# Key parts stored once each, and the cyclic row of key parts made by five loads an operand instead of three loads from a doubled store

## The chip, the cores and the metric

The kernel runs on one core of a Trainium2 chip. The metric is the device time of one execution in microseconds, the median of several runs. A DMA is issued by an engine's queue (here nearly always SyncE's, "SPq" in the profile) and carried by the core's 16 DMA engines.

## The reference

One pre-norm decoder layer on x of [1, 1024, 128], with a context of [1, 6404, 128]:

```python
x = x + attn(layernorm(x))          # 16 heads of 8; k and v through a latent of 32; scores times
                                    # exp(-0.01*|t_q - t_k|), softmax, times v, times W_o
x = x + xattn(layernorm(x), ctx)    # q = x W^T + b; softmax(q ctx^T + (1 - mask) * -1e6) ctx
x = x + ffn(layernorm(x))           # fp4 block quantization of activations and weights, silu gate
```

The change lies in the first of the three. There q and k for all 16 heads are needed as operands of score matmuls with float32-like precision.

## The kernel before, in words

**Operands in three parts.** Queries and keys are scaled by a growing or a falling exponential of the position, so that the decay becomes a plain product on one side of the diagonal. This gives four operands: lower queries QL, lower keys KL, upper queries QU and upper keys KU. Each is split into three bf16 parts (high, middle, low), called parts 0, 1 and 2. One matmul over 112 partitions then multiplies a row of nine blocks of 8 partitions on either side: query parts 0,1,2 three times over against key parts in the cyclic order 0,1,2, 1,2,0, 2,0,1. The head dimension is 8, so a part of one head is 8 partitions, nine blocks are 72 partitions, and the rest hold constants and, later, three rows of softmax shifts.

**Through DRAM.** VectorE and ScalarE make the parts with (head, dimension) on 128 partitions, in the order KL, QL, QU, KU (lines 720, 733, 737, 537, 541). `store_parts` writes them to DRAM (`key_parts`, `query_parts`; lines 287 and 292). `load_operand(g, w)` (line 310) reads them back for a group g of four heads, now with 8 partitions a part and four heads times 1024 positions, 8 KB, along each partition. `load_first_queries` (line 321) does that for QL of group 0 in two halves of 512 positions. Two operand buffers alternate over the four groups. All of these are issued on SyncE's queue in the order in which the code is written; the waits there are on semaphores of the parts, of the stores' landing, and, for groups 2 and 3, on the scores of the group before last.

**Keys.** A load of 24 partitions takes three consecutive slots of `key_parts`. So that the cyclic order can be read this way, the DRAM tensor has five slots with parts 0,1,2,0,1: parts 0 and 1 are written twice. The three loads begin at slots 0, 1 and 2.

**What follows.** TensorE's first use of an operand is `max_unit(mu)`: for 16 units a half group (4 heads by 4 query tiles), in order of mu from 0 to 127, it computes 128x1024 scores (line 918), and VectorE multiplies them by the decay and takes the row maximum (line 744). The first 23 units run before any attention probability is made; with them TensorE also transposes the context (line 1051). From then on 32 "pairs" of score blocks, exponentials (ScalarE, line 609) and products with v (line 1027) run, each with four more units of maxima woven in. Units 0 to 31 are of group 0, 32 to 63 of group 1, and so on. The maxima of 16 units become shifts, stored by six small DMAs into the query operands (`load_shift`, line 335). Cross-attention and the feed-forward part come after all that.

TensorE waits for the first operands on one semaphore, `s_op0`: the three loads of KL and the three of QL's first half, 16 counts each.

Of the kernel before, what the change touches and what calls it, by code (L numbers as in the profile page):

```python
# [11 lines left out]
BF16 = mybir.dt.bfloat16  # L12
# [5 lines left out]
HEADS = 16  # L18
# [2 lines left out]
LN_EPS = 1e-5  # L21
BLOCK = 16
PARTS = 3
SLOTS = 2 * PARTS - 1
CLEAR_ROW = 64
ONES_PAIR = 1.0 + 127.0 * 2.0 ** -16
MATH_ROWS = 112
# [2 lines left out]
HG = 4  # L30
# [3 lines left out]
def decoder_layer(nc, x, ctx, mask, w_q, w_k, w_v, w_o, w_down_kv, w_up_k, w_up_v,  # L34
                  xw, xb, w_gate, w_up, w_down, out):
    S, D = x.shape[1], x.shape[2]
# [3 lines left out]
    HD = D // HEADS  # L40
    NT = S // P
    NG = HEADS // HG
    NH = S // BANK
# [31 lines left out]
    with ExitStack() as stack:  # L75
# [3 lines left out]
        def sem(name):  # L79
            return stack.enter_context(nc.semaphore(name))  # L80

        PS = stack.enter_context(nc.psum_tensor("banks", [P, 8, BANK], F32))

        k_scratch = nc.dram_tensor("key_parts", [2, SLOTS, HD, HEADS, S], BF16, kind="Internal").ap()
        q_scratch = nc.dram_tensor("query_parts", [2, NH, PARTS, HD, HEADS, BANK], BF16, kind="Internal").ap()

        ident = sb("ident", [P, P])
# [21 lines left out]
        with ExitStack() as first_stack:  # L109
            def sb0(name, shape, dt=F32):  # L110
                return first_stack.enter_context(nc.sbuf_tensor(name, shape, dt))
# [4 lines left out]
            parts_sb = sb0("operand_parts", [P, 4, PARTS, S], BF16)  # L116
# [8 lines left out]
        NB = 2  # L125
# [20 lines left out]
        def operand(buf, which):  # L146
            return ops[buf][:, which, :, :]
        QL, KL, QU, KU = range(4)
# [3 lines left out]
        def queries(buf, which, half):  # L152
            return ops[buf][:, which, :, :].rearrange("p h n -> p (h n)").rearrange(
                "p (a h n) -> p a h n", a=NH, h=HG)[:, half, :, :]
# [55 lines left out]
        s_op = [[sem(f"lower_operands_loaded_{b}") for b in range(NB)], [sem(f"upper_operands_loaded_{b}") for b in range(NB)]]  # L210
# [28 lines left out]
        def unit(b, i):  # L239
            half, pair, odd = b // NT, b % NT // 2, b % 2  # L240
            head = i // 2 + 2 * ((i + odd) % 2)
            on = i % 2 == 0
            return head, (half if on else 1 - half) * TPB + pair, half
# [3 lines left out]
        def max_slot(mu):  # L247
            return (mu + max(mu - 1, 0) // UNITS) % 2
# [10 lines left out]
        def chunk(c):  # L259
            return c * BANK, min(BANK, S2 - c * BANK)  # L260
# [15 lines left out]
        def _(sp):  # L276
# [5 lines left out]
            def store_parts(w):  # L282
                if w in (KL, KU):
                    for part, ready in ((0, s_hi), (1, s_mid), (2, s_lo)):
                        sp.wait_ge(ready, NH * (turn_of(w) + 1))
                        for slot in range(part, SLOTS, PARTS):
                            sp.dma_start(k_scratch[w // 2, slot].rearrange("d h n -> (d h) n"),
                                         parts_sb[:, w, part, :]).then_inc(s_scr[w], 16)
                    return
                for half in range(NH):  # L290
                    sp.wait_ge(s_lo, NH * turn_of(w) + half + 1)
                    sp.dma_start(q_scratch[w // 2, half].rearrange("a d h n -> (d h) a n"),
                                 parts_sb[:, w, :, half * BANK:(half + 1) * BANK]).then_inc(
                                     s_scr0 if w == QL and half == 0 else s_scr[w], 16)

            def load_operand(g, w):
                if g == 0:
                    sp.wait_ge(s_scr[w], 16 * (SLOTS if w in (KL, KU) else 1 if w == QL else NH))
                if g < NB:
                    sp.wait_ge(s_spare[g], 2 + 2 * g)  # L300
                if g == 0 and w in (QL, QU):
                    sp.wait_ge(s_qz, 2)
                for s in range(PARTS):
                    rows = operand(g % NB, w)[s * PARTS * HD:(s + 1) * PARTS * HD, :, :]
                    if w in (KL, KU):
                        src = k_scratch[w // 2, s:s + PARTS, :, g * HG:(g + 1) * HG].rearrange("a d h n -> (a d) h n")
                    else:
                        rows = rows.rearrange("p h n -> p (h n)").rearrange("p (a m) -> p a m", a=NH)
                        src = q_scratch[w // 2, :, :, :, g * HG:(g + 1) * HG].rearrange("f a d h n -> (a d) f (h n)")
                    sp.dma_start(rows, src).then_inc(s_op0 if g == 0 and w == KL else s_op[w // 2][g % NB], 16)  # L310

            def load_first_queries(half):
                sp.wait_ge(s_spare[0], 2)
# [44 lines left out]
            for hg in range(3, NG * NH):  # L358
                if hg % NH == 1 and hg // NH + 1 < NG:
                    g = hg // NH + 1  # L360
# [9 lines left out]
            for t in range(NT + 1):  # L370
                for m in range(NMP if t < NT else 0):
                    n = t * NMP + m
# [6 lines left out]
                    w = min(MP, S2 - m * MP)  # L379
# [127 lines left out]
        def _(act):  # L507
# [49 lines left out]
            def mem_high(c):  # L557
                k0, kw = chunk(c)
                act.wait_ge(s_mt, c + 1)
                if c == 0:  # L560
                    act.wait_ge(s_scr0, 16)
                    for w in range(4):
                        act.wait_ge(s_scr[w], 16 * (SLOTS if w in (KL, KU) else 1 if w == QL else NH))
                act.activation(memT_hi[:, k0:k0 + kw], PS[:, c % 4, 0:kw], ACT.Copy).then_inc(s_mhi, 1)

            def mem_low(c):
# [349 lines left out]
        def _(pe):  # L916
            def mm(o, a, b, start=True, stop=True, alone=False):
                return pe.matmul(o, a, b, start=start, stop=stop, skip_group_check=alone)  # L918
# [38 lines left out]
            def max_unit(mu):  # L957
                hg, h = mu // UNITS, mu % UNITS // TPB
                g, qt = hg // NH, hg % NH * TPB + mu % TPB
                if hg >= 1 and mu % UNITS == 1:  # L960
                    pe.wait_ge(s_mxd, mu)
                elif hg >= 1 and mu % UNITS == 2:
                    pe.wait_ge(s_sp, hg)
                elif mu >= 2:
                    pe.wait_ge(s_mxd, mu - 1)
                if mu % UNITS == 0 and hg % NH == 0:
                    if hg == 0:
                        pe.wait_ge(s_op0, 16 * 2 * PARTS)
                    else:
                        pe.wait_ge(s_op[0][g % NB], 16 * 2 * PARTS * (g // NB + 1) - (16 * PARTS if g % NB == 0 else 0))  # L970
                    pe.wait_ge(s_spare[g % NB], 2 + 2 * (g % NB))
                if mu == UNITS:
                    pe.wait_ge(s_op[0][0], 16 * PARTS)
                ql, kl = queries(g % NB, QL, hg % NH), operand(g % NB, KL)
                j = mu % TPB
                for i in range(NH):
                    last = mm(PS[:, 4 + 2 * max_slot(mu) + i, :], ql[0:MATH_ROWS, h, j * P:(j + 1) * P],
                              kl[0:MATH_ROWS, h, i * BANK:(i + 1) * BANK])
                last.then_inc(s_mx, 1)
# [5 lines left out]
            def scores(n, j):  # L985
                u = n * PU + j
                gb = 2 * n + j // HG % 2
                g, b = gb // BLKS, gb % BLKS
                if j == 0 and gb % NT == 0:
                    hg = gb // NT  # L990
                    if b == 0:
                        pe.wait_ge(s_op[1][g % NB], 16 * 6 * (g // NB + 1))
                    pe.wait_ge(s_sh[hg % 2], 16 * 2 * PARTS * (hg // 2 + 1))
                if u >= 3:
                    pe.wait_ge(s_p, u - 2)
                bank = PS[:, u % 3, :]
                half = b // NT
                def side(kq, h, kt, cols, **more):
                    qs, ks = (QL, KL) if kq == "lower" else (QU, KU)
                    return mm(bank[:, cols] if kq != "diag" else bank[:, h * P:(h + 1) * P],  # L1000
                              operand(g % NB, ks)[0:FULL_ROWS, h, kt * P:(kt + 1) * P],
                              queries(g % NB, qs, half)[0:FULL_ROWS, h, cols], **more)
                if j == 2 * HG:
                    kt = half * TPB + b % NT // 2
                    d0 = kt % TPB * P
                    for h in range(HG):
                        last = side("diag", h, kt, slice(d0, d0 + P), start=(h == 0), alone=True)
                elif j % 2 == 1:
                    h, kt, _ = unit(b, j % HG)
                    last = side("lower" if kt < half * TPB else "upper", h, kt, slice(0, BANK))  # L1010
                else:
                    h, kt, _ = unit(b, j % HG)
                    d0 = kt % TPB * P
                    last = side("lower", h, kt, slice(d0, BANK))
                    if d0 > 0:
                        last = side("upper", h, kt, slice(0, d0), start=False, alone=True)
                last.then_inc(s_st, 1)
# [218 lines left out]
            for t in range(NT):  # L1236
                for c in range(NC):
                    probs_T(t, c)
                    n = (t + 1) * NC + LEAD + c
# [36 lines left out]
```

## Time and profile before

| | us |
|---|---|
| median of 3 runs (564.05 to 565.44) | 564.52 |
| the profiled execution | 563.12 |
| its span, in which all times below stand | 561.0 |
| TensorE busy in the span | 494.5 (88%) |
| VectorE busy | 366.3 (65%) |
| ScalarE busy | 334.5 (60%) |

Times in the profile are counted from the span's start. "Idle before" an instruction is put down to what ended it. A DMA's time is that of its issue on the queue; its data moves later. "DMA share" is the mean busy share of the 16 DMA engines in a stretch, GB/s what they moved. KB of a DMA are 1024 bytes: a load of 24 partitions by 8 KB is listed as 192.0 KB.

### The profile page before, as it was taken

How to read it: one execution, taken by the hardware profiler on the slowest of the kernel's cores; microseconds unless marked ns; L12 is line 12 of the kernel's file. 1: busy time of each engine (PE TensorE's matmuls, PEld its weight loads, DVE VectorE, ACT ScalarE, POOL GpSimd, SP SyncE). 2: the span in 40 equal slices, each digit the busy share in tenths (PEclk: the TensorE clock that was granted, in tenths of full speed). 3: DMA queues.
4: the chain of work that ended last, by engine and by line, in shares of the span. 5: the costliest groups of instructions: out<-in, count | busy, mean ns of one | idle time of the engine just before them, and what ended most of it. 6: DMA issues, size and time to landing. Idle time of an engine off the chain costs nothing.

```text
span 561.0 us, 9555 instructions
## 1 busy us (share of the span) xinstructions
PE 494.5 (88%) x3394; PEld 319.8 (57%) x3394; DVE 366.3 (65%) x874; ACT 334.5 (60%) x659; POOL 169.9 (30%) x283
## 2 busy tenths in 40 slices
PE   6539899999999999999879979799897997989953
PEld 5305433333333333323659979799797997878841
DVE  7789988888778878701674366646566565653543
ACT  3545777787878777889155827446272653628410
POOL 7800033544444453233443221312222132110000
PEclk9857999999999999999989989989899999989985
DMA  8787300052007000063565323233332434300000
GB/s 239 236 265 150 84 4 2 4 114 58 1 3 160 13 2 2 1 176 100 188 215 156 109 75 115 90 112 91 112 115 61 124 99 122 90 1 6 1 5 5
DMA packets 21810, 49.19 MB, mean 88 GB/s; under 512 B 3948, under 2 KB 9268, under 8 KB 21188
## 3 DMA queue, kind: packets, MB, share of 16 engines
q1 hardware_dynamic: 21012, 47.87, 30.3%
q8 instruction: 27, 0.44, 0.3%
q0 software_dynamic: 224, 0.54, 0.3%
q10 hardware_dynamic: 528, 0.18, 0.2%
q14 instruction: 19, 0.16, 0.1%
HBM read 43.67 MB, written 4.72 MB: 86 GB/s over the span
## 4 chain that ended last, share of the span: by engine, by line
PE 68%; DVE 21%; DMA 3%; issue 3%; ACT 2%; POOL 1%; SPq 1%; DVEq 0%; ACTq 0%; POOLq 0%
PE banks L918 47%; PE banks L1027 11%; PE banks L1172 6%; DVE banks L744 6%; DVE logits L825 3%; PE banks L1038 2%; DMA mring<-in_mask_BxSxS_ik 1%; DVE fa L861 1%; ACT probs L609 1%; DMA operands<-query_parts 1%; DMA x_sb<-in_x 1%; DVE xn L709 1%; PE banks L1220 1%; DVE qc_lo L791 1%; DVE fa L860 1%
## 5 line engine op out<-in xcount | busy, mean ns | idle before, releaser
L609 ACT ACTIVATE probs<-banks 128x512 f32<-128x512 f32 x288 | 158.9, 600 | 40.6 <-PE banks L918 34.8
L744 DVE CUSTOM_DVE_ANT_0 banks<-banks,decay 128x1024 f32<-128x1024 f32 x128 | 155.0, 1245 | 30.4 <-PE banks L918 29.8
L918 PE MATMUL banks<-operands 112*128 112x512 bf16 (+4 forms) x736 | 147.4, 332 | 20.9 <-DMA operands<-query_parts 13.5
L918 PEld LDWEIGHTS banks<-operands 115*128 115x128 bf16 (+1 forms) x736 | 55.1, 98 | 126.8 <-ACT probs L609 57.5
L918 PEld LDWEIGHTS banks<-mem,pT 128*128 128x128 f32 (+1 forms) x816 | 109.3, 197 | 7.9
L918 PE MATMUL banks<-mem,pT 128*128 128x128 f32 (+1 forms) x816 | 112.9, 282 | 0.0
L825 DVE CUSTOM_DVE_ANT_0 logits<-banks,mring 128x512 f32<-128x512 f32 (+1 forms) x102 | 67.5, 668 | 49.3 <-PE banks L918 25.0
L630 ACT ACTIVATE pT<-banks 128x512 f32<-128x512 f32 (+1 forms) x104 | 60.4, 580 | 53.0 <-PE banks L1172 53.0
L484 POOL TENSOR_SCALAR mring<-mring 128x1024 f32<-128x1024 int32 (+1 forms) x55 | 52.8, 959 | 85.1 <-DMA mring<-in_mask_BxSxS_ik 82.7
L465 POOL TENSOR_SCALAR_AFFINE_SELECT probs<-probs 128x128 f32<-128x128 f32 x128 | 37.1, 293 | 113.4 <-ACT probs L609 111.8
L1027 PE MATMUL banks<-probs,v_ext 128*32 128x512 f32 x512 | 68.2, 604 | 0.7 <-ACT probs L609 0.5
L918 PE MATMUL banks<-memT_hi,qc_hi 128*128 128x512 f32 (+1 forms) x104 | 50.0, 481 | 19.1 <-DVE cmax L825 19.1
L1172 PE MATMUL banks<-ident,logits 128*128 128x128 f32 (+1 forms) x408 | 63.7, 279 | 0.0
L620 ACT ACTIVATE logits<-logits,neg_max 128x1024 f32<-128x1024 f32 (+1 forms) x56 | 58.8, 1050 | 6.7 <-DVE neg_max L832 6.7
L1172 PEld LDWEIGHTS banks<-ident,logits 128*128 128x128 f32 (+1 forms) x408 | 49.8, 144 | 4.0 <-issue 2.2
L457 POOL TENSOR_TENSOR rstd<-mv,half_neg 128x1 f32<-128x1 f32 x16 | 8.8, 550 | 127.1 <-DVE mv L867 85.2
L918 PE MATMUL banks<-memT_hi,qc_lo 128*128 128x512 f32 (+1 forms) x104 | 41.5, 399 | 0.0
L918 PE MATMUL banks<-memT_lo,qc_hi 128*128 128x512 f32 (+1 forms) x104 | 41.0, 394 | 0.0
L918 PEld LDWEIGHTS banks<-memT_hi,qc_hi 128*128 128x128 f32 x104 | 20.7, 199 | 22.3 <-DVE cmax L825 21.6
L469 POOL TENSOR_SCALAR_AFFINE_SELECT probs<-probs 128x512 f32<-128x512 f32 x32 | 20.3, 635 | 41.1 <-ACT probs L609 41.1
L650 ACT ACTIVATE xqT<-banks 128x128 f32<-128x128 f32 x8 | 2.2, 277 | 37.9 <-PE banks L1209 37.9
L918 PEld LDWEIGHTS banks<-memT_hi,qc_lo 128*128 128x128 f32 x104 | 20.2, 194 | 4.4
(168 smaller groups left out, 482.4 us busy)
## 6 DMA issues: line engine op xcount, KB each, us to landing
mring<-in_mask_BxSxS_ik SPq DMA_DIRECT2D x47, 512.0 KB, 3.5
operands<-key_parts SPq DMA_DIRECT2D x24, 192.0 KB
operands<-query_parts SPq DMA_DIRECT2D x21, 192.0 KB
key_parts<-operand_parts SPq DMA_DIRECT2D x10, 256.0 KB, 3.7
query_parts<-operand_parts SPq DMA_DIRECT2D x4, 384.0 KB, 4.5
mring<-in_mask_BxSxS_ik SPq DMA_DIRECT2D x8, 130.0 KB, 2.3
operands<-shift_parts SPq DMA_DIRECT2D x48, 4.0 KB, 1.8
operands<-query_parts SPq DMA_DIRECT2D x6, 96.0 KB
```

The lines of the kernel that those rows point to most:

```text
L465: pool.affine_select(out=diag, in_=diag, compare_op=ALU.is_ge, fill=0.0, base=0, pattern=[[1, P]], channel_multiplier=-1).then_inc(s_sel, 1)
L469: pool.affine_select(out=upper, in_=upper, compare_op=ALU.is_ge, fill=0.0, base=-1, pattern=[[0, HG], [-1, P]], channel_multiplier=1).then ...
L484: pool.tensor_scalar(src.bitcast(F32), src, -1.0, -NEG, ALU.add, ALU.mult).then_inc(s_ma, 1)
L609: act.activation(probs[:, to, :], PS[:, u % 3, :], ACT.Exp).then_inc(s_p, 1)
L620: act.activation(y, y, ACT.Exp, bias=neg_max[:, t:t + 1], accum_out=esum[:, t, e:e + 1]).then_inc(s_e, 1)
L630: last = act.activation(pT[:, n % 3, 0:o], PS[:, 2 + n % 2, 0:o], ACT.Copy)
L744: dve.tensor_tensor_reduce(out=rows, in0=rows, in1=decay[:, off:off + S], scale=1.0, scalar=-3.0e38, op0=ALU.mult, op1=ALU.max, accum_out= ...
L825: dve.tensor_tensor_reduce(out=logits_sb(t)[:, k0:k0 + kw], in0=PS[:, logits_bank(n), 0:kw], in1=mk, scale=1.0, scalar=-3.0e38, op0=ALU.ad ...
L918: return pe.matmul(o, a, b, start=start, stop=stop, skip_group_check=alone)
L1027: last = pe.matmul(PS[h * VW:(h + 1) * VW, 3, :], v_ext[:, kt, g * HG + h, :], probs[:, (gb % 2) * HG + i, :], start=(b % NT == 0), stop=( ...
L1038: last = pe.matmul(PS[h * VW:(h + 1) * VW, 3, d0:d0 + P], v_ext[:, kt, g * HG + h, :], probs[:, 2 * HG + n % 2, h * P:(h + 1) * P], start= ...
L1172: last = pe.transpose(PS[0:kw, 2 + n % 2, j * P:(j + 1) * P], logits_sb(t)[:, k * P:k * P + kw], ident[:, :])
```

## The change

`key_parts` has three slots, one a part, and each part is stored once: for KL and KU three stores of 256 KB each where there were five. In `load_operand` for keys, the row of nine blocks is made by five loads: (row 0, parts 0,1,2), (row 24, parts 1,2), (row 40, part 0), (row 48, part 2), (row 56, parts 0,1). They fill 24, 16, 8, 8 and 16 partitions. Loads of queries stay as they are. The counts waited for are changed to match (8 loads for a pair of operands instead of 6).

```diff
 PARTS = 3
-SLOTS = 2 * PARTS - 1
+K_RUNS = ((0, 0, 3), (24, 1, 2), (40, 0, 1), (48, 2, 1), (56, 0, 2))
+LOADS = len(K_RUNS) + PARTS
...
-        k_scratch = nc.dram_tensor("key_parts", [2, SLOTS, HD, HEADS, S], BF16, kind="Internal").ap()
+        k_scratch = nc.dram_tensor("key_parts", [2, PARTS, HD, HEADS, S], BF16, kind="Internal").ap()
...
                         sp.wait_ge(ready, NH * (turn_of(w) + 1))
-                        for slot in range(part, SLOTS, PARTS):
-                            sp.dma_start(k_scratch[w // 2, slot].rearrange("d h n -> (d h) n"),
-                                         parts_sb[:, w, part, :]).then_inc(s_scr[w], 16)
+                        sp.dma_start(k_scratch[w // 2, part].rearrange("d h n -> (d h) n"),
+                                     parts_sb[:, w, part, :]).then_inc(s_scr[w], 16)
...
+                heads = slice(g * HG, (g + 1) * HG)
+                if w in (KL, KU):
+                    for row, part, n in K_RUNS:
+                        sp.dma_start(operand(g % NB, w)[row:row + n * HD, :, :],
+                                     k_scratch[w // 2, part:part + n, :, heads].rearrange("a d h n -> (a d) h n")).then_inc(
+                                         s_op0 if g == 0 and w == KL else s_op[w // 2][g % NB], 16)
+                    return
                 for s in range(PARTS):
-                    rows = operand(g % NB, w)[s * PARTS * HD:(s + 1) * PARTS * HD, :, :]
-                    if w in (KL, KU):
-                        src = k_scratch[w // 2, s:s + PARTS, :, g * HG:(g + 1) * HG].rearrange("a d h n -> (a d) h n")
...
-                        pe.wait_ge(s_op0, 16 * 2 * PARTS)
+                        pe.wait_ge(s_op0, 16 * LOADS)
```

On SyncE's queue, at the stores of KL and the first loads, these rows stood before (a row is line, destination <- source, partitions x elements, and how many in a row):

```order
L287 DMA key_parts<-operand_parts 128x1024 x5
L292 DMA query_parts<-operand_parts 128x3x512 x2
L310 DMA operands_0<-key_parts 24x4096 x3
L321 DMA operands_0<-query_parts 24x2048 x6
L292 DMA query_parts<-operand_parts 128x3x512 x2
```

and these now:

```order
L287 DMA key_parts<-operand_parts 128x1024 x3
L292 DMA query_parts<-operand_parts 128x3x512 x2
L306 DMA operands_0<-key_parts 24x4096
L306 DMA operands_0<-key_parts 16x4096
L306 DMA operands_0<-key_parts 8x4096 x2
L306 DMA operands_0<-key_parts 16x4096
L325 DMA operands_0<-query_parts 24x2048 x6
L292 DMA query_parts<-operand_parts 128x3x512 x2
```

Two stores are gone, and two more DMAs stand between the stores and the query loads; the order of everything else is the same.

On the same queue, at the loads of group 2 between the shifts of two half groups, there stood before:

```order
L335 DMA operands_1<-shift_parts 1x16x128 x6
L310 DMA operands_0<-key_parts 24x4096 x3
L310 DMA operands_0<-query_parts 24x2x2048 x6
L310 DMA operands_0<-key_parts 24x4096 x3
L335 DMA operands_1<-shift_parts 1x16x128 x6
```

and now:

```order
L339 DMA operands_1<-shift_parts 1x16x128 x6
L306 DMA operands_0<-key_parts 24x4096
L306 DMA operands_0<-key_parts 16x4096
L306 DMA operands_0<-key_parts 8x4096 x2
L306 DMA operands_0<-key_parts 16x4096
L312 DMA operands_0<-query_parts 24x2x2048 x6
L306 DMA operands_0<-key_parts 24x4096
L306 DMA operands_0<-key_parts 16x4096
L306 DMA operands_0<-key_parts 8x4096 x2
L306 DMA operands_0<-key_parts 16x4096
L339 DMA operands_1<-shift_parts 1x16x128 x6
```

Twelve loads have become sixteen, with the same bytes to the same partitions; the next group's shifts stand behind them as before.

## Rows read from the trace of the kernel before

**Rows 1.** The page: span and busy time of each engine.

```profile
span 561.0 us, 9555 instructions
PE 494.5 (88%) x3394; PEld 319.8 (57%) x3394; DVE 366.3 (65%) x874; ACT 334.5 (60%) x659; POOL 169.9 (30%) x283
```

**Rows 2.** The chain that ended last, 24 to 37 us: start, duration, what.

```profile
24.58 1.30 DVE operand_parts L737 x2
...
25.90 0.36 SPq L292
...
26.37 0.55 SPq L310
...
26.96 0.98 SPq L310
...
27.99 0.37 SPq L310
...
29.22 6.00 DMA operands<-query_parts
35.23 0.24 issue
...
36.64 1.23 DVE banks L744
```

**Rows 3.** The chain, 60 to 68 us.

```profile
65.69 1.12 DVE banks L744
...
66.93 1.04 PE banks L918 x4
```

**Rows 4.** TensorE's waits, 20 to 70 us: total, times, longest.

```profile
PE banks L918 <- DMA operands<-query_parts: 13.5, 1, 13.5
```

**Rows 5.** Busy time in stretches: each engine's, then PEclk, DMA share, GB/s.

```profile
4.00:12.00 8.00, 6.48 (x38) 5.44 (x36) 6.21 (x22) 4.67 (x10) 6.17 (x4) 1.00 1.09 290
...
25.00:26.00 1.00, 0.00 (x0) 0.00 (x0) 1.00 (x3) 0.14 (x1) 1.00 (x1) 1.00 0.00 0
36.00:38.00 2.00, 1.35 (x5) 0.16 (x3) 1.53 (x4) 0.00 (x0) 0.00 (x0) 0.50 1.07 379
43.00:46.00 3.00, 2.65 (x6) 0.49 (x5) 3.00 (x5) 0.00 (x0) 0.00 (x0) 0.50 0.82 161
57.00:58.00 1.00, 0.77 (x5) 0.33 (x4) 0.97 (x4) 1.00 (x3) 0.00 (x0) 1.00 0.00 0
119.00:131.00 12.00, 12.00 (x92) 4.24 (x87) 9.76 (x16) 9.74 (x18) 5.07 (x11) 1.00 0.75 165
```

**Rows 6.** SyncE's queue in order of time: start, duration, issues.

```profile
19.81 2.77 SPq L287 DMA_DIRECT2D key_parts<-operand_parts  x5
25.29 0.97 SPq L292 DMA_DIRECT2D query_parts<-operand_parts  x2
26.37 1.99 SPq L310 DMA_DIRECT2D operands<-key_parts  x3
28.47 2.34 SPq L321 DMA_DIRECT2D operands<-query_parts  x6
31.61 0.99 SPq L292 DMA_DIRECT2D query_parts<-operand_parts  x2
...
42.16 2.34 SPq L310 DMA_DIRECT2D operands<-key_parts  x6
44.54 1.19 SPq L310 DMA_DIRECT2D operands<-query_parts  x3
58.60 3.79 SPq L335 DMA_DIRECT2D operands<-shift_parts  x6
```

**Rows 7.** SyncE's queue, 115 to 190 us.

```profile
116.12 1.11 SPq L310 DMA_DIRECT2D operands<-key_parts  x3
117.69 2.38 SPq L310 DMA_DIRECT2D operands<-query_parts  x6
...
168.63 1.11 SPq L310 DMA_DIRECT2D operands<-key_parts  x3
169.78 2.43 SPq L310 DMA_DIRECT2D operands<-query_parts  x6
```

**Rows 8.** Line 744 alone from 36 us on (two instructions a unit).

```profile
36.00:131.40 95.40, 78.67 (x128) 0.94 0.34 82
36.00:131.60 95.60, 78.79 (x129) 0.94 0.34 82
```

**Rows 9.** The same to 184 us.

```profile
36.00:183.90 147.90, 118.91 (x192) 0.96 0.29 70
36.00:184.10 148.10, 119.02 (x193) 0.96 0.29 69
```

**Rows 10.** All waits of TensorE, 110 to 190 us.

```profile
PE banks L918 <- DVE row_max L744: 2.0, 4, 0.5
```

More of the change, by code:

```diff
@@ L297, in load_operand @@
                 if g == 0:
-                    sp.wait_ge(s_scr[w], 16 * (SLOTS if w in (KL, KU) else 1 if w == QL else NH))
+                    sp.wait_ge(s_scr[w], 16 * (PARTS if w in (KL, KU) else 1 if w == QL else NH))
                 if g < NB:
@@ L302, in load_operand @@
                     sp.wait_ge(s_qz, 2)
-                for s in range(PARTS):
-                    rows = operand(g % NB, w)[s * PARTS * HD:(s + 1) * PARTS * HD, :, :]
-                    if w in (KL, KU):
-                        src = k_scratch[w // 2, s:s + PARTS, :, g * HG:(g + 1) * HG].rearrange("a d h n -> (a d) h n")
[L307 to L310, printed above, removed]
+                heads = slice(g * HG, (g + 1) * HG)
[5 more added lines that the diff above has]
+                    return
+                for s in range(PARTS):
+                    rows = operand(g % NB, w)[s * PARTS * HD:(s + 1) * PARTS * HD, :, :].rearrange("p h n -> p (h n)")
+                    sp.dma_start(rows.rearrange("p (a m) -> p a m", a=NH),
+                                 q_scratch[w // 2, :, :, :, heads].rearrange("f a d h n -> (a d) f (h n)")).then_inc(
+                                     s_op[w // 2][g % NB], 16)
             def load_first_queries(half):
@@ L562, in mem_high @@
                     for w in range(4):
-                        act.wait_ge(s_scr[w], 16 * (SLOTS if w in (KL, KU) else 1 if w == QL else NH))
+                        act.wait_ge(s_scr[w], 16 * (PARTS if w in (KL, KU) else 1 if w == QL else NH))
                 act.activation(memT_hi[:, k0:k0 + kw], PS[:, c % 4, 0:kw], ACT.Copy).then_inc(s_mhi, 1)
@@ L967, in max_unit @@
                     if hg == 0:
-                        pe.wait_ge(s_op0, 16 * 2 * PARTS)
+                        pe.wait_ge(s_op0, 16 * LOADS)
                     else:
-                        pe.wait_ge(s_op[0][g % NB], 16 * 2 * PARTS * (g // NB + 1) - (16 * PARTS if g % NB == 0 else 0))
+                        pe.wait_ge(s_op[0][g % NB], 16 * LOADS * (g // NB + 1) - (16 * len(K_RUNS) if g % NB == 0 else 0))
                     pe.wait_ge(s_spare[g % NB], 2 + 2 * (g % NB))
@@ L991, in scores @@
                     if b == 0:
-                        pe.wait_ge(s_op[1][g % NB], 16 * 6 * (g // NB + 1))
+                        pe.wait_ge(s_op[1][g % NB], 16 * LOADS * (g // NB + 1))
                     pe.wait_ge(s_sh[hg % 2], 16 * 2 * PARTS * (hg // 2 + 1))
```

## The prediction

> **What bounds the kernel now.** I read the page first: TensorE is busy for 494.5 of 561.0 us [rows 1], so over most of the span a DMA costs nothing. Then the chain of work that ended last, because the changed DMAs matter only where it passes through them. It does so once. From 24.58 us on it runs through the last splits of QL on VectorE, the issue of the query stores, the three KL loads and the first query loads on SyncE's queue, and then 6.00 us of DMA, up to 35.23 [rows 2]. The table of waits says the same from TensorE's side: 13.5 us idle before its first score matmul, ended by the query loads, its only wait for a DMA between 20 and 70 us [rows 4]. From 36.64 us to 66.8 the chain is VectorE's maxima of line 744, one unit after the other, and then it is TensorE's [rows 2, 3]. So whatever moves the landing at 35.23 moves the rest of the kernel by as much: the units behind it are bound by VectorE, TensorE's work by their order, and nothing is made in advance meanwhile.
>
> **The removed stores.** Two stores of KL are gone from the issue at 19.81 [rows 6]. What did they hold up? Between 25 and 26 us the DMA engines moved nothing, share 0.00 [rows 5]: all five stores had drained before the first query store (issued 25.29) reached them, and that one waits for VectorE's split, not for the queue. The first KL load follows the second query store (25.90 + 0.36) at 26.37 with no wait for the landing of the key stores in between [rows 2]. So the two stores are worth 0 here. Without that cover (stores still draining at 25.3) they would be worth up to 2 x 262 kB at 379 GB/s, the rate of the store stretch at 36 to 38 us [rows 5], 1.4 us. The two stores of KU do lie in busy DMA time, and their 1.4 us lets the KU loads start earlier, but no one waits for those.
>
> **The two more issues an operand.** An issue of such a load takes 2.34 / 6 = 0.39 us (six from 42.16) [rows 6], so the query loads are issued 0.8 us later, from 29.3 instead of 28.47. The data of KL takes 3.6 us (below) and starts after the query stores' data, hence the query loads are issued well before their turn. Worth 0, and 0.8 us if there were no queue of data. Behind them on SyncE stands the store of QU, issued at 31.61; the last query load would now end at 30.81 + 0.8 = 31.6, just in time.
>
> **The five loads themselves.** This is the term that decides. The rows to read are the stretches with their DMA share. In 119 to 131 us only loads of 24 partitions are in flight: share 0.75, so about 12 of 16 engines are busy, and 165 GB/s; at 43 to 46 us it is 161 GB/s [rows 5]. A busy engine thus moves 165 / 12 = 13.7 GB/s. It is not that an engine can't do more: stores from all 128 partitions ran at 379 GB/s, 23.7 an engine, loads to 128 partitions (x and the context, 4 to 12 us) at 290, 18.1 an engine. What differs is the number of partitions that are written, so I read the 165 GB/s as 24 partitions at 6.9 GB/s each. By that a load of 8 KB a partition takes 196.6 kB / 165 GB/s = 1.19 us whether it has 24, 16 or 8 partitions, as long as loads go one after the other: three loads take 3.6 us, five take 6.0. **+2.4 us** on KL, and the first queries land behind it.
>
> The Trainium skill (SBUF — State Buffer, Door 1: The DMA port swizzle) states what would make this so: four neighbouring partitions, and the four 32 further on, share one of 16 ports of about 27 GB/s. By it 24 partitions have six ports, 163 GB/s, and the traces agree with 165 and 161; 8 partitions have two ports, 54 GB/s, so 65.5 kB take 1.2 us, and the sum would again be +2.4.
>
> Both ends for this term. Low: loads overlap, because an engine that is through with its rows goes on to the next load, which writes other partitions. If overlap were perfect the bytes are the same and the term is 0 (it could be -0.5 if the four engines idle before now carry rows of the 16-partition loads; more is excluded, since the low rate is not the engines'). High: engines get out of step, and the query loads behind, 0.6 us each by their 98 kB, suffer as well; doubling three of them adds 1.8, together +4.2. I take 2.4, since the measured loads before show no overlap: sustained over 12 us they never exceed the rate of one [rows 5].
>
> **Later loads.** Groups 2 and 3 are loaded under TensorE's work, and TensorE waits for no DMA in 110 to 190 us [rows 10]. Group 2: issue from 116.12 [rows 7]; six loads of KL and QL at 1.19 are 7.1 us, with about 2 us ahead of and behind the data some 125.3. They are needed at unit 64, which VectorE starts at 131.5 [rows 8] and TensorE about 1 us before: 5 us of margin. With the change KL costs 2.4 more, or 4.8 if QU's loads, running past QL's on engines that are ahead, slow QL by as much again: 0.2 to 2.6 us of margin stay. Group 3 is the same: issue 168.63, unit 96 at 184.0 [rows 7, 9]. Worth 0; if the cover is gone, 0.5 to 1.5 us each. The shifts of the first half group are issued at 58.60, with the DMA engines idle from 57 on [rows 5, 6]; KU and KL of the next group push that data 4.8 us later, plus 2.4, less 1.4 for KU's stores, to about 62.5, while the shifts are issued 61.0 to 64.8. The last of the six still finds the engines free. Worth 0.
>
> **Sum.** 0 + 0 + 2.4 + 0. The profiled execution took 563.12 (span 561.0 and 2.1 around it): 565.5. It lies 1.4 below the median of the runs, so I forecast 564.5 + 2.4 = **566.9**. What a measurement of this kernel tells from no change is 0.3%, 1.7 us.
>
> **Rivals.**
> - *Rows an engine, not partitions, set the time* (not slower). If the 12 busy engines carry two rows of 8 KB each of a 24-partition load, a load of 16 or 8 partitions gives an engine one row. Then the most loaded engines have 2 + 1 + 1 + 1 + 1 = 6 rows, as before with three loads of 2, and the time of KL is 3.6 us in both kernels. For it: the share of exactly 0.75. Against it: the 23.7 and 18.1 GB/s of an engine in other stretches. It decides if a row keeps taking 1.19 / 2 = 0.6 us in an 8-partition load; the time is 564.5. The Trainium skill (DMA: Bandwidth & Descriptors, Why a DMA increments its semaphore by 16 and not by 1) has this split: the number of engines is the largest up to 16 that divides the slowest dimension, 12 for 24 partitions, 16 for 16, 8 for 8; the share of 0.75 agrees. Taken alone it gives 564.5. 24%.
> - *The crowding spreads* (slower still). The query loads run out of step, +4.2, and the loads of groups 2 and 3 come 0.5 late each: 564.5 + 5.2 = 569.7. For it: margins of 0.2 to 2.6 us. Against: 5 us of margin before. 16%.
> - *The idle engines help.* The 16-partition loads use all 16 engines and the term is -0.5, with KU's stores gone too: 564.0. Against it: the rate of 24 partitions did not come from the engines. 10%.
> - The forecast itself, +1.2 to +3.5: 50%.
>
> **Chances and range.** Slower by over 0.3% (over 566.2): nearly all of the forecast's half and of the second rival, 0.61. Within: the first rival, the low edge of the forecast, most of the third, 0.33. Faster: 0.06, from the third and scatter. The range reaches from just under the first and third rivals, 564.1, to just over the second, 570.0.
>
> **What the profile of the changed kernel would show.** TensorE's wait before the first score matmul grows from 13.5 to about 15.9 us, line 744 begins at about 39.0 instead of 36.64, and the chain's DMA piece there is longer by 2.4 us. In the stretch from 29 to 34 us, GB/s falls well below 165, and the DMA share with it or not: a share that stays up at falling GB/s says that engines stand in line for partitions. The DMA engines are still idle between 25 and 26 us. No wait of TensorE for a DMA in 110 to 190 us. I am wrong if KL's data takes 3.6 us again (first rival), or if the maxima show a stall at units 64 or 96 (second).

## The result and the profile after

| | before | with the change |
|---|---|---|
| median of 20 runs each, us | 564.05 | 566.64 |
| ratio, 95% interval | | 1.004 (1.0025 to 1.0054) |
| span of the profiled execution, us | 561.0 | 565.4 |

The change costs 0.4%, by the ratio 2.3 us (1.4 to 3.0 by the interval); the two medians are 2.6 us apart. The spans differ by more than that, 4.4 us, and single executions of one kernel scatter by as much: the 20 runs of before lie between 560.55 and 566.65.

The page's sections on DMA show what was moved: 46.83 MB on SyncE's queue where before had 47.87, two parts less for KL and for KU, in 16 loads of 128 KB, 8 of 192 KB and 16 of 64 KB for the keys.

```profile
span 565.4 us, 9567 instructions
...
q1 hardware_dynamic: 20628, 46.83, 32.5%
...
HBM read 43.67 MB, written 3.67 MB: 84 GB/s over the span
...
operands<-key_parts SPq DMA_DIRECT2D x16, 128.0 KB
key_parts<-operand_parts SPq DMA_DIRECT2D x6, 256.0 KB, 3.4
...
operands<-key_parts SPq DMA_DIRECT2D x8, 192.0 KB
...
operands<-key_parts SPq DMA_DIRECT2D x16, 64.0 KB
```

SyncE's queue in order of time answers to [rows 6] (start, duration, issues; the key loads are line 306 now):

```profile
20.12 2.43 SPq L287 DMA_DIRECT2D key_parts<-operand_parts  x3
25.61 0.97 SPq L292 DMA_DIRECT2D query_parts<-operand_parts  x2
26.68 2.64 SPq L306 DMA_DIRECT2D operands<-key_parts  x5
29.43 2.35 SPq L325 DMA_DIRECT2D operands<-query_parts  x6
```

The chain that ended last, in 24 to 41 us, answers to [rows 2], and TensorE's first wait, in the second fence, to [rows 4]. The last two have TensorE's first score matmul, in before and in the change:

```profile
30.19 6.81 DMA operands<-query_parts
37.00 0.24 issue
...
38.41 1.23 DVE banks L748
```

```profile
PE banks L922 <- DMA operands<-query_parts: 14.9, 1, 14.9
```

```profile
35.47 1.87 PE L918 MATMUL banks<-operands 112*128 112x512 bf16 x4 [13.47 <-DMA operands<-query_parts]
```

```profile
37.25 1.86 PE L922 MATMUL banks<-operands 112*128 112x512 bf16 x4 [14.94 <-DMA operands<-query_parts]
```

In this execution all of the start is 0.3 us late (first query store at 25.61 against 25.29). Counted from that issue, the first operands land 11.4 us later against 9.9 before: 1.5 us more. The stretches, with DMA share and GB/s at the end, show why; the second fence has before from 31 to 35 us.

```profile
25.00:26.00 1.00, 0.00 (x0) 0.00 (x0) 1.00 (x2) 0.46 (x1) 1.00 (x1) 0.50 0.00 0
29.00:31.00 2.00, 0.00 (x0) 0.00 (x0) 1.04 (x2) 2.00 (x2) 0.00 (x0) 0.50 1.06 221
31.00:33.00 2.00, 0.00 (x0) 0.00 (x0) 1.67 (x3) 1.76 (x4) 0.00 (x0) 0.50 0.72 98
33.00:35.00 2.00, 0.00 (x0) 0.00 (x0) 2.00 (x4) 1.78 (x5) 0.00 (x0) 0.50 0.83 146
...
121.00:131.00 10.00, 10.00 (x76) 3.31 (x74) 7.63 (x12) 8.32 (x16) 3.94 (x10) 1.00 0.78 113
```

```profile
31.00:33.00 2.00, 0.00 (x0) 0.00 (x0) 2.00 (x4) 1.78 (x5) 0.00 (x0) 0.50 0.77 174
33.00:35.00 2.00, 0.00 (x0) 0.00 (x0) 1.81 (x4) 1.84 (x4) 0.00 (x0) 0.50 1.03 252
```

At 31 to 33 us as many engines are busy as before (0.72 against 0.77), but they move 98 GB/s instead of 174. I read busy engines at a falling rate as engines that stand in line; the experiments bear on that. The same is seen for group 2 at 121 to 131 us, 113 GB/s at a share of 0.78, where [rows 5] have 165 at 0.75; there it costs nothing, since TensorE has no wait for a DMA from 60 to 190 us (all its waits there):

```profile
PE banks L922 <- DVE row_max L748: 3.0, 7, 0.5
PE banks L922 <- ACT memT_lo L573: 0.5, 1, 0.5
```

Line 748 (line 744 before) begins at 38.41 against 36.64, 1.8 us later, and its last unit at 237.35 against 234.79, 2.6 us later. The 0.8 us in between arose at units 10 and 11 and is told under the last heading. The other 1.8 us of the 4.4 between the two spans arise behind the last unit and were not followed.

### The profile page after: what moved, and what is told of

It is laid out like the page before. It is cut to its first block, busy times and chain, and to the rows that moved or that the text cites. A ratio compares the mean times of both kernels' runs of the same rounds, so it can differ in the third digit from the quotient of the medians.

```text
span 565.4 us, 9567 instructions
## 1 busy us (share of the span) xinstructions
PE 495.8 (88%) x3394; PEld 320.9 (57%) x3394; DVE 367.4 (65%) x874; ACT 334.6 (59%) x659; POOL 168.6 (30%) x283
## 3 DMA queue, kind: packets, MB, share of 16 engines
q1 hardware_dynamic: 20628, 46.83, 32.5%
## 4 chain that ended last, share of the span: by engine, by line
PE 69%; DVE 22%; issue 3%; ACT 2%; DMA 2%; POOL 1%; SPq 1%; DVEq 0%; ACTq 0%; POOLq 0%
PE banks L922 47%; PE banks L1031 11%; PE banks L1176 6%; DVE banks L748 5%; DVE logits L829 2%; PE banks L1042 2%; DVE fa L865 1%; DMA operands<-query_parts 1%; ACT probs L613 1%; DVE xn L713 1%; DVE fa L864 1%; DVE fa L860 1%; DVE xn L874 1%; PE banks L1224 1%; DVE f_small L856 1%
## 5 line engine op out<-in xcount | busy, mean ns | idle before, releaser
L922 PE MATMUL banks<-operands 112*128 112x512 bf16 (+4 forms) x736 | 147.9, 332 | 22.3 <-DMA operands<-query_parts 14.9
```

## The experiments

Behind each ratio stands a time from the kernel's profile: from the issue of the first query store to TensorE's first score matmul. It is 25.29 to 35.47, 10.2 us, in before, and 25.61 to 37.25, 11.6 us, in the change.

**The five loads with the doubled stores.**

```diff
-                        sp.dma_start(k_scratch[w // 2, part].rearrange("d h n -> (d h) n"),
-                                     parts_sb[:, w, part, :]).then_inc(s_scr[w], 16)
+                        for slot in range(part, SLOTS, PARTS):
+                            sp.dma_start(k_scratch[w // 2, slot].rearrange("d h n -> (d h) n"),
+                                         parts_sb[:, w, part, :]).then_inc(s_scr[w], 16)
```

> The five loads of the change for every key operand, but the five stores of before (parts 0 and 1 twice). If the five loads are the whole cost, as predicted, this is 2.4 us slower than before (ratio 1.004) and the same as the change, since the removed stores are worth nothing. If the stores were worth something that the change gets back, this kernel is slower than the change by up to 1.4 us. If rows an engine set the time, it is as fast as before.

Measured: 1.0048 (1.0028 to 1.0068), 12.3 us. The five loads without the single stores have the loss of the whole change.

**Three loads with the single stores.**

```diff
-                        src = k_scratch[w // 2, s:s + PARTS, :, g * HG:(g + 1) * HG].rearrange("a d h n -> (a d) h n")
+                        src = k_scratch[w // 2, 0:PARTS, :, g * HG:(g + 1) * HG].rearrange("a d h n -> (a d) h n")
```

> The three stores of the change with three loads of 24 partitions as before. Each of the three loads takes parts 0, 1, 2, so the key row is 0,1,2 three times and the products of parts are not those of the reference; bytes, shapes and places of the loads are those of before. My theory: no stores are on the path, so the time is that of before within 0.3 us, and the DMA engines are idle before the first query store in both. Rival: the two stores of KL are worth something, up to 1.4 us faster.

Measured: 0.999 (0.9971 to 1.0009), 11.1 us. The stores are worth nothing that the ratio shows, but its interval still holds a gain of 1.6 us and so doesn't exclude the rival. The traces do. In this kernel and in the one with five loads and doubled stores the first query store was issued at 24.30 us, 1 us sooner than in before. With doubled stores the DMA engines were still busy at 24 to 25 us (share 0.80, against 0.01 here), and yet from 25 to 26 us the two are nearly alike, 0.79 and 264 GB/s against 0.78 and 259: the query store's data began to move in the same quarter of a microsecond, after 25.0 us, in both.

**Five loads for KL of group 0 alone, and for all but it.** The stores are doubled, and a load of three parts from slot 1 or 2 is one of before's. The second kernel has the two lists exchanged.

```diff
+K_FIRST = ((0, 0, 3), (24, 1, 2), (40, 0, 1), (48, 2, 1), (56, 0, 2))
+K_REST = ((0, 0, 3), (24, 1, 3), (48, 2, 3))
...
-                    for row, part, n in K_RUNS:
+                    for row, part, n in K_FIRST if g == 0 and w == KL else K_REST:
```

> Doubled stores as before and three loads everywhere, except for KL of group 0, which takes the five loads. My theory: the whole loss lies here, ratio 1.004, TensorE's first wait for a DMA about 1.5 us longer than before. Rival (the crowding spreads to the later loads): this kernel loses less than the change, by 1 us or more. If rows an engine set the time: as before.

> Doubled stores as before, three loads for KL of group 0 and five for the seven other key operands. My theory: all of these lie under other work, ratio 1.000, the first wait for a DMA as before, and no wait for a DMA at units 32, 64 or 96. Rival (the crowding spreads): slower by 1 us or more, with stalls at those units.

Measured: 1.0057 (1.0036 to 1.0078) and 12.4 us with the five loads at the first KL alone; 1.0005 (0.9984 to 1.0026) and 9.5 us with them at the seven others. No loss outside the first operand's loads can be told from 0, and the seven others are hidden. In the second kernel TensorE's waits from 60 to 190 us again have no DMA among them.

**Nine loads of 8 partitions for the first KL.**

```diff
-K_FIRST = ((0, 0, 3), (24, 1, 2), (40, 0, 1), (48, 2, 1), (56, 0, 2))
+K_FIRST = ((0, 0, 1), (8, 1, 1), (16, 2, 1), (24, 1, 1), (32, 2, 1), (40, 0, 1), (48, 2, 1), (56, 0, 1), (64, 1, 1))
```

> As the kernel before, but KL of group 0 by nine loads of 8 partitions. If 8 partitions are written at the rate of 8/24 of 165 GB/s, nine loads take 10.8 us instead of 3.6 when they follow one another, so the first operands land up to 7 us later than before, ratio up to 1.012. If rows an engine set the time (one row of 8 KB on each of 8 engines, 0.6 us a load), nine take 5.4 us: 1.8 us later, ratio 1.003. In the stretch behind the first load the DMA moves about 55 GB/s by the first, 110 by the second.

Measured: 1.0087 (1.0046 to 1.0127), and 24.33 to 39.00, 14.7 us: 4.5 us more than before. That is between the two expectations. So is the rate, 98 and 111 GB/s where I had 55 for loads in line:

```profile
28.00:30.00 2.00, 0.00 (x0) 0.00 (x0) 0.80 (x2) 2.00 (x3) 0.89 (x1) 0.50 0.58 98
30.00:32.00 2.00, 0.00 (x0) 0.00 (x0) 1.91 (x4) 1.76 (x5) 0.00 (x0) 0.50 0.66 111
```

Neither reading is complete. Six more loads cost 4.5 us, 0.75 us each, where the prediction's rule of 1.19 us a load gives 7.2. Either these loads overlap in part, or 8 neighbouring partitions alone take more than 55 GB/s; no run here has such a load by itself, so that stays open. The rate also doesn't tell the time of an engine's row from a limit at the partitions. The next kernel tells these two apart.

**Five loads spread over the partitions.** Sizes and number of loads stay those of the change, and the profile counts the same packets on SyncE's queue as with five contiguous loads for the first KL, 21036. What is changed is which partitions a small load writes, and with it how long its issue takes (all five: 3.54 us instead of 2.64).

```diff
-K_FIRST = ((0, 0, 3), (24, 1, 2), (40, 0, 1), (48, 2, 1), (56, 0, 2))
+K_FIRST = ((slice(0, 24), 0, 3), (slice(24, 72, 3), 1, 2), (slice(26, 72, 6), 0, 1), (slice(29, 72, 6), 2, 1), (slice(25, 72, 3), 0, 2))
```

> As the kernel before, but KL of group 0 by five loads of 24, 16, 8, 8 and 16 partitions, where the four smaller ones are written to every third or sixth partition of 24 to 71 (together they cover each once). The blocks of the key row stand in another order, so products of parts are not those of the reference. Sizes, counts and issues are those of the change. If what counts is the number of partitions a load writes, this is as slow as five contiguous loads: 1.5 to 2.4 us later than before. If neighbouring partitions share a way in, the loads now use up to four times as many ways and the first operands land as early as before, within 0.5 us; VectorE isn't ready for them earlier than 0.5 us before that, so no more can be won.

Measured: 0.9998 (0.9977 to 1.002), 26.58 to 37.31, 10.7 us. The loss is gone. The stretches keep near the rate of three loads. Counted from the first query store, 32 to 34 us here is 31 to 33 in the change: 176 GB/s against 98.

```profile
30.00:32.00 2.00, 0.00 (x0) 0.00 (x0) 0.80 (x3) 1.86 (x3) 0.00 (x0) 0.50 0.81 202
32.00:34.00 2.00, 0.00 (x0) 0.00 (x0) 1.90 (x5) 1.90 (x4) 0.00 (x0) 0.50 0.84 176
```

So it isn't the number of partitions of a load either, as I had put it: it is that they are neighbours. In this execution the first query store was issued about 1 us late and VectorE's splits ended at 38.0, so the first unit began at 38.48, no sooner than in the change; the gain is read from the ratio and from the count.

**Nine loads spread over the partitions.**

```diff
+K_FIRST = ((slice(0, 72, 9), 0, 1), (slice(1, 72, 9), 1, 1), (slice(2, 72, 9), 2, 1), (slice(3, 72, 9), 1, 1), ...)
```

(The five others begin at partitions 4 to 8 in the same way.)

> As the kernel with nine loads of 8 partitions for KL of group 0, but each load writes every ninth partition of 0 to 71 instead of 8 neighbours. Same sizes, issues and number of partitions a load; the order of the key row's blocks is another, so products of parts are not those of the reference. If neighbouring partitions share a way in, the nine loads no longer stand in line: from the first query store to TensorE's first score matmul about 10.5 us instead of 14.7 with nine contiguous ones, ratio about 1.001. If an engine's nine rows or the nine issues cost the time, it stays near 14 us and 1.008.

Measured: 1.0049 (1.0024 to 1.0073), and 25.41 to 38.06, 12.7 us. I expected 10.5: half missed. The queue shows why:

```profile
26.49 6.01 SPq L309 DMA_DIRECT2D operands<-key_parts  x9
32.61 2.58 SPq L328 DMA_DIRECT2D operands<-query_parts  x6
```

```profile
30.00:32.00 2.00, 0.00 (x0) 0.00 (x0) 1.90 (x4) 1.76 (x5) 0.00 (x0) 0.50 0.34 102
```

An issue to partitions that are not neighbours took 6.01 / 9 = 0.67 us, where nine contiguous ones took 3.76 / 9 = 0.42. Now SyncE's issues are most likely the bound: the DMA engines are busy for 0.34 of 30 to 32 us and still move the 102 GB/s for which the contiguous loads needed 0.66. An engine moves 102 / (0.34 x 16) = 18.8 GB/s, against 111 / (0.66 x 16) = 10.5. From the end of the last key issue to the first score matmul it is 38.06 - 32.50 = 5.6 us, against 39.00 - 29.17 = 9.8 with contiguous loads. The data part is as expected; the issue was what I left out.

**GpSimd's memsets held back.** The profiles so far had shown something else in this stretch (last heading): VectorE's line 727, the argument of the decay table, took between 1.3 and 2.8 us.

```diff
+            pool.wait_ge(s_iota2, 1)
             for w, value in ((KL, ONES_PAIR), (QL, 0.0), (QU, 0.0), (KU, ONES_PAIR)):
                 pool.memset(spare_rows(1, w), value).then_inc(s_spare[1], 1)
```

> The kernel before, with GpSimd's four memsets of the second operand buffer held back until VectorE has made the decay argument (line 727). In the profiles so far that instruction ends at 27.1 us when it starts before the fourth memset and at 28.85 when it doesn't, 1.75 us later, whatever the loads; the maxima start behind VectorE's splits. If this pair of times is a wait of VectorE for GpSimd's memset, the instruction now takes 1.3 us or less in every execution, VectorE is ready for the first unit at 35.5 or earlier, and since the first operands land at 35.2 the median falls by 0.3 to 1 us. Rival: it is something else, and the time is that of before.

Measured: 1.0011 (0.999 to 1.0032), 9.7 us. The instruction took 1.15 us, so the wait was for the memset; the gain I expected didn't come. VectorE's last split before the maxima ends at 34.83 + 1.29 = 36.1, not at 35.5, and the first unit begins at 36.26 against 36.64.

**The change with heads in pairs.** Keys and queries of heads 0 and 1 come first, those of 2 and 3 behind them on a semaphore of their own, which TensorE waits for at unit 8.

```diff
-            load_operand(0, KL)
-            load_first_queries(0)
+            for pair in range(2):
+                load_first_keys(pair)
+                load_first_query_heads(pair)
...
+                if mu == UNITS // 2:
+                    pe.wait_ge(s_op0b, 16 * LOADS)
```

> The change, with the first group's lower keys and first half of queries loaded for heads 0 and 1 first and for heads 2 and 3 behind them, on a semaphore of its own that TensorE waits for at unit 8. The first eight loads carry half the bytes: if the crowded loads cost what they cost by their bytes, the first operands land about 3 us sooner than in the change, VectorE becomes what the first unit waits for, and the time is that of before or up to 0.5 us less (ratio 0.999 to 1.000). If the loss of the change were elsewhere, it would stay at 1.004.

Measured: 0.9995 (0.9974 to 1.0015). TensorE's first score matmul begins at 34.42 us, 2.8 sooner than in the change. By the profile its wait no longer ends with a DMA, and VectorE goes from its last split (36.59 + 1.29) to its first unit without a wait:

```profile
PE banks L943 <- ACT xwT L580: 12.1, 1, 12.1
```

```profile
37.80 1.23 DVE L769 CUSTOM_DVE_ANT_0 banks<-banks,decay 128x1024 f32<-128x1024 f32 x1
```

This undoes the loss with all five loads in place: not because they take less, but because the first unit no longer waits for all of them.

**Head pairs and late memsets, with three loads and with five.** The edits are the two above, on the kernel before and on the change.

> The kernel before with both: loads in head pairs and memsets held back. The first operands land at about 32.7 us instead of 35.2, VectorE is ready at about 35.2 at the latest, so the maxima begin 1.2 to 2 us earlier than in before: ratio 0.997. If VectorE's splits alone set the start, the same with three or five loads.

> The change with both. Theory: the five loads are now hidden behind VectorE's splits, so the time is that of the kernel before with both, ratio 0.997, and the change costs nothing any more. Rival: the second pair of heads, 1.5 us later than with three loads, is missed at unit 8, and it is slower by some tenths of a us up to 1 us.

Measured: 1.0007 (0.9987 to 1.0028) and 1.0003 (0.9983 to 1.0023). With three loads as with five the first unit begins at 36.2 and 36.0 us, and unit 8 is not late with either. They are equal, as the theory says, but the 0.3% over before that I expected isn't there. The first score matmul came at 32.8 us with three loads, as expected; but VectorE's last split ended at 36.3 us, not at 35.2. The waits of VectorE for the first operands were only 0.5 us in before; that is all that better loads can win, and here it was not measurable. I found no version that is faster than before.

## Why the prediction was right

- **The removed stores, 0.** Right: the DMA engines are idle at 25 to 26 us in both, single stores alone give 0.999, and where the first query store came 1 us sooner, doubled stores still didn't delay its data.
- **Two more issues an operand, 0.** Right in the change: the query loads are issued 0.65 us later after the first query store than before (0.8 was forecast), and the loads spread over the partitions, whose issues take 0.9 us longer still, have no loss. The spread nine loads show the condition under which it fails.
- **The five loads, +2.4 us.** The profiled execution of the change shows +1.5, the two kernels with the same five loads and doubled stores +2.1 and +2.2 by the same count; the mean of the three is 1.9. The four kernels with three contiguous loads for the first KL (before, single stores, five loads for all but the first, late memsets) lie at 9.5 to 11.1, so one of these counts is good to about 1 us, and it is the ratios that settle the size: 1.004, 1.0048 and 1.0057, or 2.3 to 3.2 us. The size was right. That the forecast of 566.9 lies within 0.3 us of the measured 566.64 is in part luck, for two premises of the term don't hold as written. The first is that loads go strictly one after the other at 1.19 us each: the nine loads should then have cost 7.2 us more and cost 4.5. The second is a rate for each partition, whichever it is. The spread loads refute that, 10.7 us and 0.9998 with 24, 16, 8, 8 and 16 partitions. The trouble is loads to a few neighbours. That neighbours share a way in explains it, and no run here shows the ways themselves. The Trainium skill (SBUF — State Buffer, Door 1: The DMA port swizzle) has it so, four neighbours and the four 32 further on at one port, and these runs agree with it as far as neighbours go: by it an 8-partition load to neighbours reaches two ports, one to every sixth partition seven or eight. What the four 32 further on do, no run here shows.
- **Nothing of it hidden.** Right within the intervals: the loads of the first KL alone have the whole loss, 1.0057.
- **Later loads, 0.** Right: 1.0005 with five loads for the seven other operands, though group 2's data ran at 113 GB/s instead of 165. The rival of spreading crowding is refuted: it wanted 1 us or more, and no unit waits for a DMA.
- **Rows an engine** as the limit is refuted as well: it has the first KL at 1.000, which was 1.0057. The third rival, a gain from the engines that were idle before, is refuted by the same ratio.
- **TensorE's first wait, 15.9.** It was 14.9 in the change's profile, and 15.6 and 15.7 in the two others with the five loads. The chain's DMA piece grew from 6.00 to 6.81 us, not by 2.4; it also began 1.0 us later, at 30.19 instead of 29.22.
- **Line 748 at 39.0.** It was 38.41, and part of that has another cause: in this execution VectorE's splits ended at 37.9, 1.7 us later than before. With the operands in time the first unit would have begun at 37.9, so 0.5 us of the 1.8 is all that the DMA held up there. That the loss is the loads' is shown by the kernel with five loads and doubled stores, in which VectorE was early: there it sat idle for 1.62 us before its first unit, against 0.47 before. With the five loads for the first KL alone it sat idle for 1.53 us, though it was late.

```profile
37.78 1.23 DVE L750 CUSTOM_DVE_ANT_0 banks<-banks,decay 128x1024 f32<-128x1024 f32 x1 [1.62 <-PE banks L924]
```

(the timeline of the kernel with five loads and doubled stores; "idle before" in brackets).

## What to carry to other kernels

A DMA's bytes do not tell its time: ask which partitions it writes, and how many loads one behind the other write only a few neighbours each. Spreading a small load over the partitions gave the time back here, at a dearer issue: 0.67 us instead of 0.42, which with nine loads became the limit. A redundant copy in DRAM that lets one load cover more partitions can be worth more than the store that it costs, where the load is waited for and the store isn't. If a wait can't be made shorter, make it wait for less: half of the heads first gave back all that was lost.

## What was not expected

**VectorE and GpSimd.** Line 727 (a tensor_scalar of 128x1920, int32 to float32; line 731 in the change) took 1.33 us in before and 2.75 us in the change, though neither the instruction nor GpSimd's code was changed. The timelines of the two, of VectorE and of GpSimd:

```profile
25.79 1.33 DVE L727 TENSOR_SCALAR decay<-iota_d 128x1920 f32<-128x1920 int32 x1
...
20.81 8.05 POOL L428 MEMSET operands<- 64x2048 f32 x4
```

```profile
26.10 2.75 DVE L731 TENSOR_SCALAR decay<-iota_d 128x1920 f32<-128x1920 int32 x1
...
20.79 7.04 POOL L432 MEMSET operands<- 64x2048 f32 x4
```

The third memset ends and the fourth begins at about 26.05 us. If VectorE's instruction began before it, the instruction ended at 27.1 and the memsets took 1.0 us longer in all; if it began after, it ended at 28.85, 1 us behind the memset's end. In the ten profiled kernels with the memsets in their place it ended six times at 27.1 to 27.2 us and four times at 28.8 to 29.0, and 0.2 us in its start decided (25.90 was early, 26.08 late). With the memsets held back it took 1.15 us:

```profile
25.93 1.15 DVE L728 TENSOR_SCALAR decay<-iota_d 128x1920 f32<-128x1920 int32 x1
...
27.14 7.04 POOL L429 MEMSET operands<- 64x2048 f32 x4 [6.38 <-DVE decay L728]
```

So one instruction waits for the other as a whole. VectorE's ended about 1.1 us behind the end of the memset that ran when it began, the third or the fourth, however early it began: at 24.79 us, in the kernel with five loads and doubled stores, it took 2.32 us and ended at 27.1 too. A chance order moved VectorE's splits by 1.7 us. How often each order comes in unprofiled runs is open; the median didn't move when it was removed.

**TensorE's clock.** After the long wait TensorE ran at half its clock, 1.2 GHz, until shortly before 48 us in before and until 52 in the change:

```profile
47.00:48.00 1.00, 1.00 (x5) 0.60 0.82 172
48.00:49.00 1.00, 1.00 (x10) 1.00 0.70 148
```

```profile
50.00:51.00 1.00, 1.00 (x5) 0.50 0.99 148
51.00:52.00 1.00, 1.00 (x7) 0.53 0.73 90
52.00:53.00 1.00, 1.00 (x8) 1.00 0.76 115
```

(TensorE alone: busy, clock, DMA share, GB/s.) From unit 8 on, the context's transposes are added to its work, and at the half clock it, not VectorE, sets the pace: units 9 and 10 begin 1.7 us apart instead of 1.2, and units 10 and 11 1.4 instead of 1.2. In before only unit 9 came so late, 1.7 us behind unit 8, as it does in the change.

```profile
49.80 1.23 DVE L748 CUSTOM_DVE_ANT_0 banks<-banks,decay 128x1024 f32<-128x1024 f32 x1 [0.42 <-PE banks L922]
51.51 1.23 DVE L748 CUSTOM_DVE_ANT_0 banks<-banks,decay 128x1024 f32<-128x1024 f32 x1 [0.42 <-PE banks L922]
```

That is the 0.8 us between the delay of the first unit and that of the last. Whether the later rise comes from the later start or from the execution is open: the kernel with three loads and single stores, whose first unit began at 36.6 like before's, also rose late, and its unit 12 began 0.8 us later than before's.
